# LSTM over gathered rows on one core: how many signals TensorE gives per chunk, and which of them frees a slot of rows

## The reference, cut to what matters

```python
seq = x[col].reshape(n, deg, d)              # 17 rows per node
def step(carry, x_t):
    h, c = carry
    gates = x_t @ w_ih.T + h @ w_hh.T + b
    i, f, g, o = jnp.split(gates, 4, axis=-1)
    c = sigmoid(f) * c + sigmoid(i) * tanh(g)
    h = sigmoid(o) * tanh(c)
```

## Time and profile before

| what | value |
|---|---|
| runs of the kernel before | 2710.15, 2723.78, 2735.73 us (median 2723.78) |
| the profiled execution's own time | 2727.58 us |
| its span, first to last instruction | 2725.8 us |
| mean granted TensorE clock | 0.881 |
| busy: PE, PEld, DVE, ACT, POOL | 2131.8, 1643.8, 1571.8, 1519.3, 1585.9 us |

### The profile page before, as it was taken

One profiled execution on the slowest core, in us unless ns is written; L12 is line 12 of the kernel. 1 busy time (PEld: TensorE's weight loads), 2 busy tenths in 40 slices (PEclk: granted clock), 3 DMA queues, 4 the chain that ended last, 5 costly groups with the idle time before them and its releaser, 6 DMA issues. The chain is left out here.

```text
span 2725.8 us, 32746 instructions
## 1 busy us (share of the span) xinstructions
PE 2131.8 (78%) x10250; PEld 1643.8 (60%) x10250; DVE 1571.8 (58%) x3518; ACT 1519.3 (56%) x4753; POOL 1585.9 (58%) x1672
## 2 busy tenths in 40 slices
PE   6488888888888888888768767777777777777776
PEld 4467767777776777767645545554554555555555
DVE  5356666666666665666735555554554555555557
ACT  3455454545455555454556656656666666666662
POOL 1666666666666666666166665665665665665660
PEclk8689999999999999898977888888887888888889
DMA  8666666666666666666111111111111111111111
GB/s 304 203 185 201 204 197 175 169 177 174 182 175 179 179 177 169 176 174 181 47 52 46 47 44 44 48 43 45 47 43 43 48 44 46 50 48 40 45 43 48
DMA packets 121049, 309.60 MB, mean 114 GB/s; under 512 B 29058, under 2 KB 42604, under 8 KB 120876
## 3 DMA queue, kind: packets, MB, share of 16 engines
q0 software_dynamic: 93264, 273.00, 36.0%
q1 hardware_dynamic: 27612, 34.51, 3.8%
HBM read 288.14 MB, written 19.26 MB: 113 GB/s over the span
## 5 line engine op out<-in xcount | busy, mean ns | idle before, releaser
L664 POOL DMA_INDIRECT sender<-table,src_index x832 | 785.8, 945 | 539.3 <-issue 286.9
L369 POOL DMA_INDIRECT shared<-gates,seq_index x833 | 789.1, 947 | 502.4 <-issue 221.2
L759 ACT ACTIVATE bank<-bank,attr 128x64 f32<-128x64 f32 x3328 | 702.3, 362 | 3.9 <-issue 3.6
L392 PE MATMUL bank<-ident,shared 128*128 128x128 f32 x3332 | 497.9, 294 | 230.7 <-DVE h_lo L467 155.2
L445 ACT ACTIVATE bank<-bank,bias 128x512 f32<-128x512 f32 (+1 forms) x663 | 401.1, 634 | 494.7 <-PE bank L404 322.9
L392 PEld LDWEIGHTS bank<-ident,shared 128*128 128x128 f32 x3332 | 425.1, 152 | 321.5 <-DVE h_lo L467 187.0
L713 PE MATMUL bank<-msg,select 128*128 128x256 f32 x1664 | 504.0, 455 | 2.1 <-DVE msg L806 2.1
L795 DVE TENSOR_TENSOR side<-sender,bank 128x192 f32<-128x192 f32 x416 | 147.0, 353 | 598.4 <-ACT bank L759 394.1
L698 PEld LDWEIGHTS bank<-a,h 64*128 64x128 f32 x1664 | 238.2, 218 | 378.9 <-issue 255.2
L698 PE MATMUL bank<-a,h 64*128 64x128 f32 x1664 | 281.1, 318 | 196.4 <-ACT bank L759 138.0
L713 PEld LDWEIGHTS bank<-msg,select 128*128 128x128 f32 x1664 | 356.8, 225 | 85.8 <-issue 9.3
(11 more groups left out here) (88 smaller groups left out, 2161.9 us busy)
## 6 DMA issues: line engine op xcount, KB each, us to landing
shared<-gates,seq_index POOLq DMA_INDIRECT x833
sender<-table,src_index POOLq DMA_INDIRECT x832
gates<-shared SPq DMA_DIRECT2D x49, 256.0 KB, 4.0
feats<-attr_in SPq DMA_DIRECT2D x13, 256.0 KB
x<-x_nodes_in SPq DMA_DIRECT2D x12, 256.0 KB
table<-up SPq DMA_DIRECT2D x12, 256.0 KB, 2.3
out<-x SPq DMA_DIRECT2D x12, 256.0 KB
shared<-x_t_in SPq DMA_DIRECT2D x3, 704.0 KB, 10.2
```

What stands on the lines that cost most here:

```text
L369: pool.indirect_dma_start(out=rows[:, k % SLOTS, j, :], out_offset=None, in_=t["gates"], in_offset=bass.IndirectOffsetOnAxis(ap=seq_index[ ...
L392: last = pe.matmul(bank[:, j * P:(j + 1) * P], rows[:, k % SLOTS, j, cols], ident[:], is_transpose=True, start=(j == 0), stop=False, skip_ ...
L664: pool.indirect_dma_start(out=sender[:, hg % 4, j, :], out_offset=None, in_=t["table"], in_offset=bass.IndirectOffsetOnAxis(ap=src_index[: ...
L759: last = act_e.activation(wy[:, j, :, k, :], w[:, 2 * i + j, :, min(k, 1), :], ACT.Copy, scale=attr[:, k, tile:tile + 1])
```

## The change

PE signals `s_gate` twice per chunk: after gates i, g and f together (q = 2), and after o (q = 3). `s_turned` is gone. ACT waits once before i, for all three gates, and once before o. POOL waits for the second signal of chunk k-5 in every step. No instruction on data is added, removed or moved.

```diff
                     for k, (step, c) in enumerate(WORK):
-                        if SLOTS <= k < NCH + SLOTS:
-                            pool.wait_ge(s_gate, 4 * (k - SLOTS + 1))
-                        elif k >= SLOTS:
-                            pool.wait_ge(s_turned, k - SLOTS + 1 - NCH)
+                        if k >= SLOTS:
+                            pool.wait_ge(s_gate, 2 * (k - SLOTS + 1))
...
-                        if step == 0:
+                        if step == 0 and q >= 2:
                             last.then_inc(s_gate, 1)
-                        elif q == 3:
-                            last.then_inc(s_turned, 1)
...
-                        last.then_inc(s_gate, 1)
+                        if q >= 2:
+                            last.then_inc(s_gate, 1)
...
                             values = banks[n % 8][:, 0:width]
-                            act_e.wait_ge(s_gate, n + 1)
+                            if q == 0:
+                                act_e.wait_ge(s_gate, 2 * k + 1)
+                            if q == 3:
+                                act_e.wait_ge(s_gate, 2 * k + 2)
```

More of the change, by code:

```diff
@@ L203, in build @@
             s_store = [sem(f"s_store{i}") for i in range(8)]
-            s_turned, s_gate, s_act = sem("s_turned"), sem("s_gate"), sem("s_act")
+            s_gate, s_act = sem("s_gate"), sem("s_act")
             s_cell, s_tanh, s_hidden = sem("s_cell"), sem("s_tanh"), sem("s_hidden")
```

## The result

| kernel | median us | lowest to highest | runs |
|---|---|---|---|
| before | 2729.76 | 2710.15 to 2760.84 | 4 |
| after | 2767.59 | 2757.25 to 2776.78 | 4 |

The ratio is 1.0162, 95% interval 1.0085 to 1.0239: slower by 38 us, 7.6 more than the 2760 of the forecast. The profiled execution has a span of 2770.5 us and a mean clock of 0.872 (before 2725.8 and 0.881).

A forecast was written before the change was run, and what follows sets the result against it. Bound: PE's signals held while POOL issues gathers, with the tanh-to-h chain behind them. Terms 0 - 0 + 37 = +37 us on 2727.58 give 2764.6, 2761 against the median, stated as 2760; range 2640 to 2805, likeliest case 2740 to 2785.

The forecast's parts named there:

- The total: Whole kernel: 2760 us, slower by 1.3%, likeliest case's own range 2740 to 2785, chance 0.42.
- Signals removed: PE, three signals fewer per chunk from step 1 on: gives back 0 us, 12 us at most by the rows.
- The hold stays: LSTM: PE's signals reach ACT 3.2 us late in some 80 chunks while POOL issues gathers; independent of signal count, so unchanged.
- ACT starts i, g and f together: ACT in chunks with late signals: chain to h starts 0.57 us later, bounds 0 and 1.4; counted through POOL's slot wait.
- Step 0: LSTM's first step: i waits for two more sets of transposes, 0.9 us, under a 5 us gather; 0 us.
- What lies behind the LSTM: Stages after the LSTM: costed at nothing, since no instruction there differs.
- The slot's signal 0.62 us late in 50 chunks: POOL's gather starts without a wait: signal moved behind o's products uses up their slack; 0.74 us each, 37 us in sum.
- Rival B: POOL: slips break its gather runs, late signals shorten, a pair's cycle is 11.0 not 11.7; -35 us, 2690; chance 0.14.
- A: LSTM: signals cause their own lateness, fewer end it wholly or half; POOL's 61.3 us a step, 2530 or 2627; chance 0.15.
- C: No change: gains and the 37 us cancel, or slips vanish in POOL's 2.0 us pause; 2725; chance 0.20.
- D: Slower by much: every stall pays a full 1.4 us item in some 80 chunks; +56 and more, 2785 up; chance 0.09.
- The signs named in advance: Profile after: POOL's second starts idle 0.6 to 0.8 us; i, g, tanh(c) back to back; h_lo waits 3.0; some 80 late chunks.

The follow-up runs named there:

- the fourth set's chip: Chip of the last two runs, signals late there: kernel before 2782.31 us; the changed kernel, unchanged, 2802.71 us, ratio 1.0066.
- the quick chip: Chip of the second set, no late signals in the changed kernel's profile: kernel before 2268.22 us; changed kernel 2273.31 us, ratio 1.0019.
- the pause: Kernel before plus two waited-for memsets on POOL ahead of each wide chunk's gathers from step 1: 2377.40 us, 1.0480; on another chip 2797.34 us, 1.0046.
- gates only: Kernel before with i, g and f sharing one signal, o apart, slot still freed after o's transposes: 2765.37 us, ratio 1.0088.
- slot only: Kernel before with the slot freed by the fourth gate signal, behind o's products, four gate signals kept: 2719.31 us, 0.9911; again 2711.34 us, 0.9937.
- the first experiments' set: First four experiments, on one chip beside 28 runs of the kernel before (median 2743.56 us): ratios 0.9911, 1.0088, 1.0087 and 1.0028.
- the kernel before once more: Kernel before, unchanged, profiled again on a third chip: 2739.29 us, ratio to itself 1.0014.

## Why the prediction was right, and where it wasn't

**The total** (2760, slower by over 1%, own range 2740 to 2785): measured 2767.59, +1.6%; on the fourth set's chip +0.7%; on the quick chip +0.2%. It came near by luck, for the sum was put together from the wrong halves. "Over 1%" itself is borne out once in three: the same waits measured 1.0162, 1.0087 and 1.0066 where signals are held.

**Signals removed, 0 us: nothing speaks against it.** Five signals with after's waits lie between the two measurements of after, and eight more cost 0.3%, with zero in the interval's reach. That bounds the term to about 1%, no closer.

**The hold stays: right.** 78 chunks after against 80. Its description, that POOL's run of gathers makes it, failed: the pause kept the hold, and the quick chip runs longer unbroken gathers with none.

**ACT starts i, g and f together, a chain 0.57 us longer: right in size.** PE's stall grew from 1.93 to 2.55 us in the mean, by 0.62, with 0.57 forecast; in gates only by 0.72. The step that failed is the one after: I let this 0.57 count only where it delayed the slot's signal. Alone it costs +22 us. It doesn't come as 0.57 in every held chunk either: of the 22 to 27 us that POOL's idle time grows in this profile, 13 to 17 lie before the first chunk of a step, 4 to 6 before the fourth and 5 to 7 before the narrow one, and the other ten chunks together have what they had.

**Step 0, 0 us: too little on chips that hold.** From its first transpose to that of step 1 it takes 74.6 to 77.7 us in the five profiles of the tables with a signal for each gate, and 81.0 to 84.5 in the four with joined gates, all on chips that hold; on the quick chip it is 62.3 with joined gates and 61.5 to 61.9 without. In the forecast's own pair this is 3.3 us. What lies behind the LSTM was put at 0 as well and took 9.9 us more in that pair; no edit touches it, and the profiles of the other kernels on chips that hold lie between 1409 and 1434 us there, so I count it as scatter.

**The slot's signal 0.62 us late in 50 chunks, +37 us: this step failed.** Alone it gives -24 and -23 us. Two things were wrong. Of the 50 starts without slack few became late: starts with up to 1 us of idle time are 105 before and 102 and 101 with the slot only. And the moved signal shortened a wait that the forecast hadn't looked at: POOL's idle time before the first chunk of a step, 40.3 and 44.8 us in 15 steps before, 20.4 and 19.8 with the slot only. PE's stalls became shorter, 1.46 us in the mean and not 1.93, but there are 95 and not 75, so that their sum gives no such gain. Rival B, with 0.14, had the direction (-35) and not the road: neither are the runs of gathers broken nor is the pair's cycle 11.0.

**The sum.** In the first experiments' set the slot gives -24 us, the gates +22, and both waits with five signals +26. What the halves leave of it, 28 us (24 by the ratios, 1.0087 less 0.9998, on 2743.56), is their meeting; it is had by subtraction and not measured for itself. After itself measured +38 and +20 (first and fourth set's chips). +37 was near as a number, by luck, and wrong as an account: the term that it stood on is -24, and the two that it lacked are +22 and about +28.

**Rivals.** A's rate without a hold, 61.3 us a step, is what POOL shows on the quick chip (61.26), by no doing of the change. C, within 1%, is what happens there, and on the fourth set's chip by its ratio of 1.0066, though not for C's reasons: on the quick chip POOL's gathers hide all but some 5 us. D, whole items lost, didn't come: the mean hold after is 2.80 us from f's product. The signs named in advance came as follows: i, g and tanh(c) back to back, yes; waits for h_lo of 3.0, in the pair shown 3.15; about 80 held, yes; POOL's second starts after 0.6 to 0.8 us, no: 7 lie between 0.36 and 1, and 24 between 1 and 1.5.

**A version that beats both.** The slot freed behind o's products, with the four gate signals kept: 0.9911 and 0.9937 of the kernel before on two chips that hold, a gain under 1%, with 1 outside both intervals. On the quick chip it wasn't run.

## What to carry to other kernels

Join signals only where nobody downstream would have begun on the first of them: here ACT lost a head start, and the ring paid for it, whatever the increments were worth. Price the two halves of a change apart before adding them, for one wait that moves can lengthen or shorten another. Sort idle time by its place in the step before trusting a mean: here all of one half's gain lay at one of thirteen chunks. And when a profile shows signals late for no reason in the program, ask for a run on a second chip before tuning against them: what costs 4.8% on one costs 0.5% on another, and the hold itself may not be there.

## What the runs showed of the hardware

The kernel before takes 2268 us on one chip and 2724 to 2782 us, by the medians, in all other sets. Of the program's work, the gathers and the pitch of the LSTM's products at full clock are as long on both; most of what differs is waiting. PE's matmuls aren't all as long: those at L713 in the edge stage take 459 ns in the mean with the changed kernel in the first set and 405 on the quick chip, with a granted clock behind the LSTM of 0.84 and 0.96. In the LSTM, steps 1 to 16 take 990 us with the changed kernel and 1208 and 1228 on the chips that hold. What lies behind it takes 1157 us on the quick chip (1115.2 to 2272.6) and 1411 (1318.9 to 2730.2) with the kernel before once more, though no instruction there differs. The waits of the edge stage from 1500 to 2100 us, first the kernel before on the chip of the forecast,

```profile
POOL sender L664 <- DVE msg L806: 125.6, 45, 8.5
...
ACT h L747 <- remote: 86.3, 28, 10.2
```

then the changed kernel on the quick chip:

```profile
ACT h L739 <- PE bank L679: 5.2, 4, 1.6
ACT h L747 <- PE bank L686: 3.4, 3, 1.2
```

ACT's h at L747 is again a consumer of PE's signal, and waits 86.3 us in 28 waits where the quick chip has 3.4 in 3. (All idle time before L747 in this window, whatever it is put down to, is 112.0 us before and 3.4 here.) So the waiting isn't the LSTM's alone. That it is the same late signal is likely and not shown, for the lateness from PE's products wasn't read in this stage. The granted clock is 0.88 there and 0.95 on the quick one; since the products' pitch in the LSTM is the same 0.23 us on both, I take the lower clock for a result of the waiting, not its cause; no run tests it. What holds the signals, and why on some chips only, stays open: it isn't their number (13 per chunk leave 82 held chunks of 3.21 us, where 5 have 80 of 3.21), nor an unbroken run of gathers. Whether it is the gathers at all, fewer transposes or another order on ACT that would end it, wasn't tried on a chip that holds.
